# A graph network on one core: a group's layer-norm statistics made one turn later, six pair places, and the span word loaded inside the pair loop

## The chip, the core and the metric

The kernel runs on one core of a Trainium2 chip. The metric is the device time of one execution in microseconds (us), the median of three runs. The engines are TensorE (PE; its weight loads are listed as PEld), VectorE (DVE), ScalarE (ACT), GpSimd (POOL) and SyncE (SP). A letter q behind an engine (DVEq, PEldq) marks what its sequencer does: register arithmetic, branches, register loads, issuing of transfers.

## What is computed

```python
agg = jax.ops.segment_sum(x[src], dst, num_segments=N)      # 6250 nodes, 200000 edges, sorted by dst
h = jax.nn.relu(agg @ W_rel + b_rel + x @ W_root)           # 256 -> 512
gates = h @ W_ih.T + b_ih + b_hh                            # 512 -> 4 * 512
i, f, g, o = jnp.split(gates, 4, axis=-1)
c = jax.nn.sigmoid(i) * jnp.tanh(g)
h_lstm = jax.nn.sigmoid(o) * jnp.tanh(c)
y = h_lstm @ W_fc + b_fc                                    # 512 -> 256
x = _layernorm(x + y, axis=-1)
```

The destinations are drawn as 6250 times a uniform number squared, so low nodes have many edges and high nodes few.

## The kernel before

**Groups and turns.** The 6250 nodes form 25 groups of 250. The program is one sequence of turns, one for each group, written once for each engine; most turns stand in a loop `period` that runs three times over six turns (turns 5 to 10, 11 to 16, 17 to 22). In turn `n` TensorE sums the neighbours of a new group, multiplies the gates of the group of turn `n-1`, and ends with `last_layer(n-1)` and the hidden layer of the new group. Each turn has four slots `j = 0..3`: `part_sum`, then `gates(n-1, j)` (24 matmuls), then the windows of the slot, or one batch of a dense product.

**Two ways of summing.** The 21 sparse groups (nodes 1000 and up) are summed from gathered rows: POOL gathers 128 rows a time (L400, four to a step, an index copied for each at L370) into a ring of `RING = 7` steps, and TensorE multiplies them by one-hots that DVE makes (`visit`, L906 and L476). A step may be overwritten only when TensorE has summed it (`steps_summed`), and summed only when it has landed (`gathered`, which SP raises at L339). The four dense groups (nodes 0 to 999) are summed from counts: their nodes form 100 windows of 10 nodes, each of two spans of 5 nodes. For each span a loop runs over the edges, 512 in an iteration. An iteration is a *pair*: DVE makes two one-hot tiles for it (`rel` L892, `hot_lo` L894, `hot_key` L897, in `span`) and TensorE multiplies the one by the other in four matmuls (L451, in `windows`). There are `PAIRS = 4` places for pairs; DVE waits for a place (`pairs_summed`), TensorE for a pair (`pairs_ready`). Spans of low nodes have several pairs, those of turns 5 and later just one.

**The span's bounds.** At each span's start both engines load one packed word of `table` into a register and split it into the loop's bounds:

```python
        def unpack(engine, regs, at):
            packed, first, past = regs
            engine.reg_load(packed, table[0:1, at:at + 1] if isinstance(at, int) else table[0:1, ds(at, 1)])
            engine.reg_alu(first, packed, PACK, ALU.python_divide)
```

The load is L299 in the profile, the arithmetic L300.

**The layer norm.** `norm_stats(n)` on DVE waits for `last_layer(n)` (`y_ready`), adds it to `x_n`, and takes mean and variance; `deviation(n)` on ACT takes the square root, for which ACT loads another table and then its old one again; `normalise(n)` on DVE scales; `store(n)` on ACT sends the rows out. `norm_stats(n - 1)` stands at the end of DVE's turn `n`, `deviation(n - 2)` at the start of ACT's turn, `normalise(n - 2)` in slot 0, `store(n - 2)` in slot 1. `load_xn` may refill `x_n` when `norm_stats` of the group before has read it (`y_sum`), which `last_layer` waits for too.

**The start.** `srcT` and `dstT` land in SBUF as int32. DVE counts edges into the table, then splits pieces of `x` into high and low parts; POOL waits for the table's head (`table_ready`), copies indices and gathers the first seven steps raw from `x` (L385), and DVE splits these too (`split_gathered`) before turn 0. No order is planned at run time: each engine does what its program lists, and waits.

## Time and profile before

| | before |
|---|---|
| median of 3 runs (lowest, highest) | 1830.2 us (1822.73, 1832.34) |
| profiled execution, its own time | 1824.41 us |
| its span | 1822.5 us |
| busy PE, POOL, DVE, ACT | 1513.5, 1281.0, 815.9, 418.5 us |
| mean granted TensorE clock | 0.91 |
| DMA | 319.14 MB, 175 GB/s on average |

The span lies 1.9 us below the execution's own time. A busy time is a sum over the whole span, and stretches with different limits stand in it side by side, so the rows below are taken by stretch.

### The profile page before, as it was taken

Reading aid. Unit: us, or ns where it says so; the run is one execution under the profiler, and the core shown is the slowest. Engines: PE = TensorE matmul, PEld = TensorE weight load, DVE = VectorE, ACT = ScalarE, POOL = GpSimd, SP = SyncE. Lnnn points to the kernel's source line nnn. Section 1 sums busy time; section 2 is a strip of 40 time slices with the busy share of each in tenths; the row PEclk is TensorE's granted clock in tenths of the full one; section 3 lists DMA queues with packets and bytes.
Section 4 is the critical chain, followed back from the end, with each engine's and each line's share of the span. In section 5 each row is a group of like instructions: output and inputs, shape, how many; then the busy total and the mean of one; then the engine's idle time right before and its main releaser. Section 6 shows DMA issues by size and latency. Waiting matters only on the chain.

```text
span 1822.5 us, 31499 instructions
## 1 busy us (share of the span) xinstructions
PE 1513.5 (83%) x6882; PEld 1213.0 (67%) x6883; DVE 815.9 (45%) x1763; ACT 418.5 (23%) x743; POOL 1281.0 (70%) x1926
## 2 busy tenths in 40 slices
PE   0157688697988898788998889899988888999997
PEld 0023355486767676667887667688876676888886
DVE  8877666431322654531324565422244654222332
ACT  0001021110112332220222333212223332222333
POOL 5875877777777877877777668776763668656640
PEclk9976677698988998889999999999998998999999
DMA  9563555576766555567766445576652455766540
GB/s 342 209 233 87 150 161 145 157 225 207 215 195 180 162 162 165 161 198 223 223 206 180 138 133 166 160 246 217 203 155 77 133 146 161 225 189 177 150 122 18
DMA packets 131966, 319.14 MB, mean 175 GB/s; under 512 B 17295, under 2 KB 68268, under 8 KB 130198
## 3 DMA queue, kind: packets, MB, share of 16 engines
q0 software_dynamic: 75264, 245.95, 46.4%
q10 hardware_dynamic: 52632, 54.80, 9.5%
q1 hardware_dynamic: 3936, 16.62, 2.4%
q8 instruction: 82, 1.34, 0.3%
q14 instruction: 52, 0.43, 0.1%
HBM read 298.10 MB, written 19.20 MB: 174 GB/s over the span
## 4 chain that ended last, share of the span: by engine, by line
PE 48%; POOL 21%; issue 19%; DVE 4%; DMA 3%; DVEq 3%; POOLq 1%; ACT 0%; ACTq 0%; SPq 0%
PE ps_blk L537 20%; POOL rows L400 14%; PE ps_agg L476 9%; PE ps_win L464 6%; POOL idx L370 6%; PE ps_y L545 4%; PE ps_blk L519 3%; PE ps_blk L524 3%; PE ps_tr L451 1%; DMA hot_key<-in_xb 1%; POOL rows L385 1%; PE ps_win L451 1%; DMA rows<-x_parts,idx 1%; POOLq L370 1%; DMA wih_sb<-in_x 1%
## 5 line engine op out<-in xcount | busy, mean ns | idle before, releaser
L400 POOL DMA_INDIRECT rows<-x_parts,idx x924 | 963.5, 1043 | 453.5 <-PE ps_agg L476 157.6
L537 PE MATMUL ps_blk<-cell,wih_sb 128*128 128x250 f32 x2400 | 545.5, 385 | 2.9 <-issue 2.2
L537 PEld LDWEIGHTS ps_blk<-cell,wih_sb 128*128 128x128 f32 x2400 | 464.1, 196 | 69.5 <-issue 8.8
L476 PE MATMUL ps_agg<-rows,onehot 128*125 x1112 | 341.8, 462 | 153.2 <-SPq L339 70.8
L476 PEld LDWEIGHTS ps_agg<-rows,onehot 128*125 128x125 f32 x1112 | 234.1, 216 | 227.5 <-issue 175.9
L906 DVE SCALAR_TENSOR_TENSOR onehot<-iota_f,tile_first,dst_u 128x500 f32 (+1 forms) x278 | 207.0, 746 | 291.7 <-PE ps_agg L476 171.6
L370 POOL COPY idx<-src_sb 128x1 int32 x956 | 264.4, 277 | 16.7 <-issue 9.7
L664 ACT ACTIVATE cell<-ps_blk,bg_sb 128x250 f32<-128x250 f32 x300 | 140.8, 470 | 544.0 <-PE ps_blk L537 470.2
L897 DVE TENSOR_TENSOR hot_key<-iota_h,rel 128x980 f16 x263 | 174.4, 663 | 0.4 <-issue 0.4
L464 PE MATMUL ps_win<-adj,hot_key 128*128 128x250 f32 x784 | 170.7, 375 | 2.4 <-DMA hot_key<-in_xb 1.5
L464 PEld LDWEIGHTS ps_win<-adj,hot_key 128*128 128x128 f32 x784 | 148.0, 190 | 21.6 <-DMA hot_key<-in_xb 4.0
L892 DVE TENSOR_SCALAR rel<-key,span_key x263 | 66.7, 254 | 186.0 <-issue 116.8
L451 PE MATMUL ps_win<-hot_key,hot_lo 128*128 x640 | 113.1, 315 | 34.4 <-issue 20.2
L894 DVE TENSOR_TENSOR hot_lo<-iota_h,src_lo 128x512 f16 x263 | 141.5, 538 | 0.3 <-issue 0.3
L451 PE MATMUL ps_tr<-hot_key,hot_lo 128*128 x412 | 83.2, 312 | 51.3 <-issue 36.3
L451 PEld LDWEIGHTS ps_win<-hot_key,hot_lo 128*128 x640 | 63.7, 100 | 78.2 <-issue 57.5
L519 PE MATMUL ps_blk<-x_t,w_sb 128*128 128x250 f32 x400 | 105.0, 398 | 0.6
L932 DVE TENSOR_TENSOR cell<-cell 128x250 f32<-128x250 f32 x100 | 42.1, 421 | 129.1 <-ACT cell L664 98.1
L451 PEld LDWEIGHTS ps_tr<-hot_key,hot_lo 128*128 x412 | 40.7, 99 | 89.0 <-issue 70.6
L937 DVE TENSOR_TENSOR cell<-cell 128x250 f32<-128x250 f32 x100 | 40.0, 420 | 124.5 <-ACT cell L657 102.8
L524 PE MATMUL ps_blk<-cell,w_sb 128*128 128x250 f32 x400 | 94.6, 378 | 0.0
L639 ACT ACTIVATE adj<-ps_win 128x490 f32<-128x490 f32 x58 | 59.7, 1029 | 146.8 <-PE ps_win L434 90.5
(125 smaller groups left out, 914.2 us busy)
## 6 DMA issues: line engine op xcount, KB each, us to landing
hot_key<-in_xb ACTq DMA_DIRECT2D x28, 896.0 KB
rows<-x_parts,idx POOLq DMA_INDIRECT x924
x_t<-in_xT ACTq DMA_DIRECT2D x25, 250.0 KB
x_n<-in_x ACTq DMA_DIRECT2D x25, 250.0 KB
out<-y ACTq DMA_DIRECT2D x25, 250.0 KB
x_parts<-wih_sb SPq DMA_DIRECT2D x4, 1024.0 KB, 6.8
wih_sb<-in_x ACTq DMA_DIRECT2D x6, 512.0 KB, 9.7
x_parts<-cell SPq DMA_DIRECT2D x2, 1024.0 KB, 7.6
```

The costliest lines, as they stand in the source:

```text
L370: g.tensor_copy(idx[:, k % RING, j:j + 1], src_sb[:, ds(chunk + j, 1)]).then_inc(idx_copied, 1)
L400: g.indirect_dma_start(rows_f[:, k * QC + j, :], None, x_parts, bass.IndirectOffsetOnAxis(ap=idx[:, k, j:j + 1], axis=0)).then_inc(landed[ ...
L451: last = mm(o, hot_lo[:, ds(half, 1), j // 2, :, j % 2].squeeze(1), hot_key[:, ds(half, 1), j // 2, :, j % 2].squeeze(1), start=False, sto ...
L464: last = mm(ps_win[:, c * GN:(c + 1) * GN], xs[:, b, c * P:(c + 1) * P], adj[:, i * X_BATCH + b, :], start=(i == 0 and b == 0 and c == 0), ...
L476: ins = mm(o, onehot[:, hot * QC + j, 0:TN], rows[:, ds(slot + j, 1), :].squeeze(1), start=(first and j == 0), stop=False)
L519: mm(ps_blk[m % BANKS][:, 0:GN], wroot_sb[:, k, m * P:(m + 1) * P], x_t[:, k, :], start=(k == 0), stop=False)
L524: last = mm(ps_blk[m % BANKS][:, 0:GN], wrel_sb[:, k, m * P:(m + 1) * P], agg_t[:, k, :], start=False, stop=(k == KI - 1))
L537: last = mm(o, wih_sb[:, k, col:col + P], h_t[:, k, :], start=(k == 0), stop=(k == KH - 1))
L664: nc.scalar.activation(dst[:, j, :], ps_blk[b % BANKS][:, 0:GN], fn, bias=bg_sb[:, bias + j:bias + j + 1]).then_inc(gate_done, 1)
L894: v.tensor_tensor(hot_lo[:, ds(half, 1), :, :, :].squeeze(1), iota_h[:, 0:P, :].unsqueeze(1).to_broadcast([P, PQ, P, 2]), src_lo[:, ds(c, ...
L897: v.tensor_tensor(hot_key[:, ds(half, 1), :, :, :].squeeze(1), iota_h[:, :, :].unsqueeze(1).to_broadcast([P, PQ, SCOLS, 2]), rel[:, ds(hal ...
L906: v.scalar_tensor_tensor(onehot[:, ds(hot, QC), 0:TN], iota_f[:, 0:TN].unsqueeze(1).to_broadcast([P, QC, TN]), nodes, dst_u[:, ds(c, QC)]. ...
```

## The change

Three edits and what they bring with them.

1. **Statistics a turn later.** On DVE `norm_stats(n - 2)` now stands in slot 0 of turn `n`, behind that slot's one-hots and windows, and `normalise(n - 2)` in slot 1. On ACT `deviation(n - 2)` and `load_xn(n - 1)` move behind slot 0, `store(n - 2)` to slot 2.
2. **Six pair places** instead of four. The room comes from the sources: `src_sb` (int32) becomes `src_u` (uint16), made by one DVE copy from a landing place in the last slot of the ring `rows`. POOL waits for that copy (`src_short`) before its first index, and in the start's seventh step for DVE's two other reads of the landing place (`src_read`).
3. **The word loaded inside the loop.** `unpack` no longer loads. Each iteration of the pair loop loads the word of the *next* span (`load_span`), on TensorE behind the fourth matmul, on DVE between `hot_lo` and the wait for `rel`; the first word is loaded before turn 0. A span with several pairs loads the same word several times.

```diff
-PAIRS = 4
+PAIRS = 6
...
-T_COLS = T_SPAN + SPANS
+T_COLS = T_SPAN + SPANS + 1
...
-        src_sb = sb("src_sb", [P, CHUNK_COLS], i32)
+        src_u = sb("src_u", [P, CHUNK_COLS], u16)
...
+        src_i = flat[:, (RING - 1) * QC * D_ROW:(RING - 1) * QC * D_ROW + CHUNK_COLS].bitcast(i32)
...
-        def unpack(engine, regs, at):
+        def load_span(engine, regs, at):
+            engine.reg_load(regs[0], table[0:1, at:at + 1] if isinstance(at, int) else table[0:1, ds(at, 1)])
+
+        def unpack(engine, regs):
             packed, first, past = regs
-            engine.reg_load(packed, table[0:1, at:at + 1] if isinstance(at, int) else table[0:1, ds(at, 1)])
             engine.reg_alu(first, packed, PACK, ALU.python_divide)
...
-            pool.wait_ge(edges_in, 32)
+            pool.wait_ge(src_short, 1)
...
             def copy_index(chunk, k, j):
-                g.tensor_copy(idx[:, k % RING, j:j + 1], src_sb[:, ds(chunk + j, 1)]).then_inc(idx_copied, 1)
+                g.tensor_copy(idx[:, k % RING, j:j + 1], src_u[:, ds(chunk + j, 1)]).then_inc(idx_copied, 1)
...
+                if k == RING - 1:
+                    pool.wait_ge(src_read, 2)
...
+            load_span(pe, pe_regs, T_SPAN)
...
-                        first, past = unpack(pe, pe_regs, at)
+                        first, past = unpack(pe, pe_regs)
                         with pe.Fori(first, past, QC):
...
                             last.then_inc(pairs_summed, 1)
+                            load_span(pe, pe_regs, at + 1)
                             next_pair(pe, pair_0, place, more_places)
...
             def turn(n, g, g1=None, g2=None, t=None, parts=ALL_PARTS, dense=False, w=None, wins=(0, 0, 0, 0), node=0, k=None, batches=()):
-                if g2 is not None:
-                    deviation(n - 2)
                 load_xt(n, g)
                 if batches:
                     load_batch(k, batches[0])
-                if g1 is not None:
-                    load_xn(n - 1, g1)
                 for j in range(KH):
...
-                    if j == 1 and g2 is not None:
+                    if j == 0 and g2 is not None:
+                        deviation(n - 2)
+                    if j == 0 and g1 is not None:
+                        load_xn(n - 1, g1)
+                    if j == 2 and g2 is not None:
                         store(n - 2, g2)
...
             dve.sem_inc(table_ready, 1)
+            dve.wait_ge(edges_in, 32)
+            v.tensor_copy(src_u[:, :], src_i).then_inc(src_short, 1)
             split_pieces(POOL_PIECES, PARTS)
...
+            load_span(dve, dve_regs, T_SPAN)
...
-                first, past = unpack(dve, dve_regs, at + T_SPAN)
+                first, past = unpack(dve, dve_regs)
...
+                    load_span(dve, dve_regs, at + (T_SPAN + 1))
                     dve.wait_ge(rel_made, s + 1)
...
                     windows_at(w, wins, j)
                     if j == 0 and back >= 2:
+                        norm_stats(n - 2)
+                    if j == 1 and back >= 2:
                         normalise(n - 2)
...
                     out_gate(n - 1, 3)
-                    norm_stats(n - 1)
...
             n = GROUPS - 1
+            norm_stats(n - 1)
             normalise(n - 1)
```

**The pair loop on TensorE**, at the step from the first span of a window to its second. MATMUL is the last or first of a pair, ISA a fused piece of register arithmetic, L306 (L311 after) advances the place. Before:

```order
L451 MATMUL ps_win<-hot_key,hot_lo 128x245
L306 ISA
L446 COMPARE_AND_BRANCH
L299 TENSOR_LOAD table
L300 ISA
L446 UNCONDITIONAL_BRANCH
L447 ISA
L451 ISA [waits pairs_ready]
```

Now:

```order
L459 MATMUL ps_win<-hot_key,hot_lo 128x245
L301 TENSOR_LOAD table
L311 ISA
L454 COMPARE_AND_BRANCH
L305 ISA
L454 UNCONDITIONAL_BRANCH
L455 ISA
L459 ISA [waits pairs_ready]
```

The load moved from behind the loop's closing branch to ahead of it, so that it runs in every iteration and not in every span.

**The pair loop on DVE**, from the second tile of a pair to the next span. Before:

```order
L894 ISA
L894 TENSOR_TENSOR hot_lo<-iota_h,src_lo 128x512
L897 ISA [waits rel_made]
L897 TENSOR_TENSOR hot_key<-iota_h,rel 128x980
L306 ISA
L888 COMPARE_AND_BRANCH
L299 TENSOR_LOAD table
L300 ISA
L888 UNCONDITIONAL_BRANCH
```

Now:

```order
L906 ISA
L906 TENSOR_TENSOR hot_lo<-iota_h,src_lo 128x512
L301 TENSOR_LOAD table
L910 ISA [waits rel_made]
L910 TENSOR_TENSOR hot_key<-iota_h,rel 128x980
L311 ISA
L900 COMPARE_AND_BRANCH
L305 ISA
L900 UNCONDITIONAL_BRANCH
```

Here the load now stands ahead of the issue of `hot_key`.

**DVE from one turn to the next**, where the turn begins with a tile's one-hots. Before, the statistics lay between the last product of a turn and the next turn:

```order
L937 TENSOR_TENSOR cell<-cell 128x250 [waits tanh_c_done]
L940 ISA
L941 TENSOR_TENSOR x_n<-x_n,bfc_sb 125x512 [waits xn_in]
L942 REGISTER_ALU
L945 ISA [waits y_free,y_ready]
L946 TENSOR_TENSOR y<-ps_y,x_n 125x512 [waits ln]
L947 REGISTER_ALU
L949 BN_STATS stats<-y 125x6 [waits y_sum]
```

Now the next turn's one-hots follow the last product at once:

```order
L950 TENSOR_TENSOR cell<-cell 128x250 [waits tanh_c_done]
L925 ISA
L925 TENSOR_LOAD table
L925 ISA x2
L927 ISA
L933 UNCONDITIONAL_BRANCH [waits hot_used]
L933 ISA
L919 ISA [waits hot_used]
L919 ISA
L919 SCALAR_TENSOR_TENSOR onehot<-iota_f,tile_first,dst_u 128x4x125
```

and the statistics stand behind the loops of the slot's spans:

```order
L900 COMPARE_AND_BRANCH
L953 ISA
L954 TENSOR_TENSOR x_n<-x_n,bfc_sb 125x512 [waits xn_in]
L958 ISA [waits y_free,y_ready]
L959 TENSOR_TENSOR y<-ps_y,x_n 125x512 [waits ln]
L960 REGISTER_ALU
L962 BN_STATS stats<-y 125x6 [waits y_sum]
```

The wait for `y_ready` has thus gone from ahead of a turn's first one-hots to behind them and the pairs.

## Rows read from the trace of the kernel before

**Rows 1.** Busy time by stretch: us, then PE, PEld, DVE, ACT, POOL, PEclk, DMA.

```profile
152.00:862.00 710.00, 582.11 (x2556) 448.58 (x2555) 317.99 (x692) 145.95 (x247) 559.29 (x845) 0.85 0.61 177
862.00:1822.00 960.00, 886.67 (x4166) 742.75 (x4166) 375.18 (x864) 268.23 (x492) 624.12 (x964) 0.96 0.56 164
```

**Rows 2.** TensorE's waits in 153 to 857 us: total, times, longest.

```profile
PE ps_agg L476 <- SPq L339: 68.1, 17, 6.0
```

**Rows 3.** POOL's waits in 862 to 1822 us.

```profile
POOL rows L400 <- PE ps_agg L476: 132.2, 18, 24.9
```

**Rows 4.** The chain that ended last, at 857 us: start, us, what.

```profile
857.29 5.11 DMA rows<-x_parts,idx
```

**Rows 5.** POOL's timeline, turn 0: start, us, instruction, idle before it.

```profile
152.43 0.97 POOL L400 DMA_INDIRECT rows<-x_parts,idx  x1 [19.43 <-PE ps_agg L476]
```

**Rows 6.** TensorE's timeline, turn 0, slot 0, and its first visit behind.

```profile
121.56 1.00 PE L451 MATMUL ps_win<-hot_key,hot_lo 128*128 x4 [0.20 <-issue]
122.74 1.00 PE L451 MATMUL ps_win<-hot_key,hot_lo 128*128 x4 [0.18 <-issue]
124.45 1.00 PE L451 MATMUL ps_win<-hot_key,hot_lo 128*128 x4 [0.71 <-DVE hot_key L897]
...
150.71 7.40 PE L476 MATMUL ps_agg<-rows,onehot 128*125 x24 [1.19 <-DVE onehot L906]
```

**Rows 7.** The pair matmuls of 110 to 150 us: count, duration min/median/max.

```profile
L451 PE MATMUL ps_win<-hot_key,hot_lo x92: 269/397/411, 109.9 to 149.1; 128*128 x92
...
L451 PE MATMUL ps_tr<-hot_key,hot_lo x32: 384/407/411, 131.0 to 140.5; 128*128 x32
```

**Rows 8.** The register loads of L299, whole span: duration ns min/median/max.

```profile
L299 DVEq TENSOR_LOAD <-table x200: 306/311/1847, 105.3 to 1526.2; - x100
L299 PEldq TENSOR_LOAD <-table x200: 296/302/323, 108.6 to 1537.9; - x100
```

**Rows 9.** The chain in 107 to 160 us, at a span's start on DVE.

```profile
119.86 0.32 DVEq L299
120.21 0.22 DVEq L300
```

**Rows 10.** DVE's timeline: first tiles of two following pairs of one span.

```profile
109.82 0.23 DVE L892 TENSOR_SCALAR rel<-key,span_key  x1
...
110.99 0.23 DVE L892 TENSOR_SCALAR rel<-key,span_key  x1
```

**Rows 11.** Costliest groups: index copies, pairs on DVE, the cast of `dstT`.

```profile
L370 POOL COPY idx<-src_sb 128x1 int32 x956 | 264.4, 277 | 16.7 <-issue 9.7
...
L897 DVE TENSOR_TENSOR hot_key<-iota_h,rel 128x980 f16 x263 | 174.4, 663 | 0.4 <-issue 0.4
...
L859 DVE CAST dst_u<-hot_key 128x1568 uint16<-128x1568 int32 x1 | 1.0, 976 | 0.2 <-DVE table L856 0.2
```

**Rows 12.** DVE's timeline, the last raw step.

```profile
101.06 0.69 DVE L772 TENSOR_SCALAR adj<-rows 128x1024 int32<-128x1024 int32 x1 [8.10 <-DMA rows<-in_x,idx]
```

**Rows 13.** TensorE's groups in 862 to 1822 us: busy, mean ns, idle before.

```profile
L451 PE MATMUL ps_tr<-hot_key,hot_lo 128*128 x176 | 32.3, 280 | 23.4 <-issue 16.0 <-DVE hot_key L897 7.4
L451 PE MATMUL ps_win<-hot_key,hot_lo 128*128 x224 | 32.1, 280 | 6.9 <-issue 4.3 <-DVE hot_key L897 2.6
```

**Rows 14.** TensorE's timeline in turns 11 and 12.

```profile
990.05 5.67 PE L476 MATMUL ps_agg<-rows,onehot 128*125 x16 [5.58 <-DVE onehot L906]
...
1031.00 0.89 PE L451 MATMUL ps_win<-hot_key,hot_lo 128*128 x4 [1.03 <-DVE hot_key L897]
...
1053.07 3.12 PE L476 MATMUL ps_agg<-rows,onehot 128*125 x12
```

**Rows 15.** DVE's timeline in the same turns.

```profile
1027.47 0.66 DVE L897 TENSOR_TENSOR hot_key<-iota_h,rel 128x980 f16 x1
...
1051.79 2.30 DVE L906 SCALAR_TENSOR_TENSOR onehot<-iota_f,tile_first,dst_u 128x500 f32 x3 [1.36 <-issue]
```

**Rows 16.** ACT's timeline in turn 10: the first of two table loads.

```profile
948.70 1.28 ACT L675 ACT_TABLE_LOAD   x1
```

More of the change, by code:

```diff
@@ L242, in gnn_kernel @@
         edges_in = sem("edges_in")
+        src_short = sem("src_short")
+        src_read = sem("src_read")
         bias_in = sem("bias_in")
@@ L316, in _ @@
             sp.dma_start(dst_next, dstq[QPC * CHUNK:(QP + 1) * QPC * CHUNK].rearrange("(p e) -> p e", p=QP)[:, 0:CHUNK]).then_inc(dstq_in, 16)
-            sp.dma_start(src_sb[:, :], srcT).then_inc(edges_in, 16)
+            sp.dma_start(src_i, srcT).then_inc(edges_in, 16)
             sp.dma_start(dst_i, dstT).then_inc(edges_in, 16)
@@ L857, in _ @@
             dve.sem_inc(spans_ready, 1)
-            dve.wait_ge(edges_in, 32)
             v.tensor_copy(dst_u[:, :], dst_i).then_inc(setup, 1)
-            v.tensor_scalar(src_part, src_sb[:, :], P - 1, None, ALU.bitwise_and).then_inc(setup, 1)
-            v.tensor_scalar(src_high, src_sb[:, :], P.bit_length() - 1, None, ALU.logical_shift_right).then_inc(setup, 1)
-            n_setup[0] += 3
+            v.tensor_scalar(src_part, src_i, P - 1, None, ALU.bitwise_and).then_inc(src_read, 1)
+            v.tensor_scalar(src_high, src_i, P.bit_length() - 1, None, ALU.logical_shift_right).then_inc(src_read, 1)
+            n_setup[0] += 1
             dve.wait_ge(setup, n_setup[0])
+            dve.wait_ge(src_read, 2)
             link(v.tensor_copy(src_lo[:, :], src_part))
```

## The prediction

> **What bounds the kernel now.** I read the busy times by stretch first, then the waits of the two engines that pass rows to each other, then the chain, and last the timelines around the edits. The reader is to see a kernel with three limits in a row.
>
> From 152 to 862 us POOL's gathering sets the pace: TensorE waits 68.1 us in 17 places for gathered steps [rows 2], and its busy time is 582.11 of 710 us [rows 1]. From 862 us on TensorE is the limit: busy 886.67 of 960 us [rows 1], while POOL waits 132.2 us for it to release the ring [rows 3]. The chain changes over at the landing of 857.29 us, which is the last gather that TensorE had to wait for [rows 4]. What a faster or slower TensorE is worth must therefore be asked twice. Before 152 us it is a third thing. POOL stands still for 19.43 us until 152.43 [rows 5], because the ring is full and TensorE is in the windows of slot 0; its next visit starts at 150.71 [rows 6]. Everything up to 862 us follows from that release, at POOL's pace. So a delay in slot 0 of turn 0 goes into the end whole; a delay in the windows of turns 1 to 8 is taken up by the waits of [rows 2]; one after 862 us counts again.
>
> What sets TensorE's pace in the windows? Within a span pairs follow at 122.74 - 121.56 = 1.18 us, and across a span's start at 124.45 - 122.74 = 1.71 us [rows 6]. The four matmuls do not explain it: they keep the array busy for 1.00 us of it, and they take 0.40 us each only because the clock is down (269 ns at best, [rows 7]). DVE does not either: the profile names `hot_key` as releaser at places, but the pair summed at 1031.00 us was made by 1027.47 + 0.66 = 1028.13 [rows 14, 15]. That leaves TensorE's own sequencer, with register arithmetic for each matmul, a branch, and at a span's start the load and the split of a word.
>
> **The load inside the loop.** The load takes 302 ns on TensorE and 311 ns on DVE, 200 times each [rows 8]. After it the next piece of arithmetic starts at 120.21, when the load of 119.86 had ended at 120.18 [rows 9]. Every load here is followed by an instruction that needs its value, so the trace cannot say whether an independent one would have passed it. I bound it: nothing at all if the sequencer goes on at once; 0.30 + 0.05 = 0.35 us each if it stands. I take the upper end, because the record of the load is a closed 0.3 us with the next record right behind it, as with any arithmetic. (Estimate: the 0.05 is the gap of 0.03 of [rows 9], rounded up for TensorE.)
>
> Loads in the loop are as many as pairs, 263 [rows 11], instead of 200. A span with one pair keeps its one load, only at the other end of the pair: no change of the sequencer's sum. A span with more pays for each further pair. In slot 0 of turn 0 there are 92 + 32 = 124 matmuls [rows 7], so 31 pairs, in 3 windows = 6 spans: 25 more loads, 25 x 0.35 = **+8.8 us**, all ahead of the release at 152.43. DVE has the same load, but its pairs follow at 110.99 - 109.82 = 1.17 us [rows 10], and part of the load falls into its wait for `rel`; at worst 1.52 against TensorE's 1.53, so it doesn't bind first. Taking the whole difference of a span's start (0.53) for a load would give 13 us, none if loads overlap 0: the ends of this term are 0 and +13.
>
> The other 63 - 25 = 38 further loads lie in the rest of turns 0 and 1, where POOL sets the pace: 38 x 0.35 = 13 us hidden by [rows 2]'s 68.1. If that cover were gone they would cost those 13.
>
> After 862 us there are 176 + 224 = 400 pair matmuls, 100 pairs, all of one-pair spans [rows 13]: 0 if the sequencer stands at a load.
>
> The Trainium skill has two sentences on such loads. "Runtime: NRT & Kernel Launch", section "Instruction fetch mechanics", gives about 200 ns for each register even in bulk, a round trip, where stores are sent off without waiting; by 200 ns the 25 loads would cost 5 us and the sum would be 6 instead of 10. No run here shows a bulk load; the single ones are at 302 ns.
>
> **The start.** DVE's copy to uint16 is put ahead of its piece work and POOL's first index waits for it. The nearest row is the cast of `dstT`, as wide: 0.98 us [rows 11]. POOL has nothing to do before its first index (9.7 us idle there, [rows 11]), and DVE stands for the raw gathers' last landing at 101.06 after 8.10 us [rows 12], so POOL's delay is the chain's: **+1.1 us** with the semaphore. Ends: 0 and +3. The index copies then read uint16 instead of int32. No row has a conversion on POOL; a copy of one column takes 277 ns [rows 11], 845/2 = 422 of them stand in the stretch where POOL is the limit [rows 1]. I take 0, since for one element a partition the data can hardly matter; a fifth more each would be 0.055 x 422 = 23 us, a doubling five times that. The wait for `src_read` comes in the seventh raw step, long after DVE's reads: 0.
>
> **Statistics a turn later.** This takes a wait and some 3 us of work on DVE from ahead of a turn's first one-hots. But TensorE doesn't stand there: it begins turn 12 at 1053.07 without idle time [rows 14], with the one-hot begun at 1051.79 and 2.30/3 = 0.77 us long [rows 15]. Its cover was thin, 0.5 us, and gets thick; worth 0 on the path. Behind the statistics in slot 0 now queue the one-hots and pairs of slot 1, but they start from a lead of six pairs, and TensorE has 24 gate matmuls ahead of it. ACT's square root brings its two table loads, 1.28 us each [rows 16], between the gates of slots 0 and 1. TensorE needs the banks of slot 1's first gate back three blocks of eight matmuls later, about 5 us, longer than 2.8: 0. `x_n` and `y` move with their readers by the same slot: 0.
>
> **Six places.** They let DVE run further ahead of a TensorE that doesn't wait for it: 0, and they are what hides the statistics.
>
> **Sum:** 8.8 + 1.1 = +9.9 us. On the profiled execution 1824.4 + 9.9 = 1834.3 us; on the median of the runs shown, 5.8 us above it, 1830.2 + 9.9 = **1840 us**. Half a per cent (9 us) is about what a measurement of this kernel tells from no change, so the forecast is a hair beyond it.
>
> **Rivals.**
> *A, loads overlap (other side).* If the sequencer issues the load and goes on, slot 0 costs nothing, and after 862 us each of the 100 pairs gets up to 0.3 us back where the sequencer is the limit. Idle before pair matmuls there is 23.4 + 6.9 = 30.3 us [rows 13]. It decides as soon as more than a third of a load is hidden there, for 100 x 0.3 = 30 outweighs 25 x 0.35. Less what the gates' queue hid already, -26: 1830 - 26 + 1 = **1805 us**. For it: the word isn't needed for a whole branch. Against it: the closed record of [rows 8, 9]. The Trainium skill's "DMA: Bandwidth & Descriptors", section "Latency and other measured facts", says that the compiler unrolls `tensor_load` fourfold to spread a floor of about 600 ns, which speaks for overlap; the trace's 302 ns is half that floor, and no run here shows two in a row.
> *B, the moved statistics do pay.* At two period starts in TensorE's stretch, such as 990.05, it stood 5.58 us with a one-hot named as releaser [rows 14]. Such a start costs 1.19 us elsewhere [rows 6]. If DVE was the reason, 2 x 4.4 = 9 us come back and nothing is left: **1831 us**, "same". Against it: it happens only where the loop `period` jumps back, and TensorE jumps there too, whatever DVE does.
> *C, the index copy is slower.* +10 and +23: **1863 us**.
> *D, statistics or square root come late*, so that `normalise` holds `cell_product` and with it ACT and the last layer: a table load of 1.28 in each of some 8 turns, **1850 us**. Against: the lead of six pairs.
>
> **How the numbers follow.** The forecast 0.45 (its own range 1833 to 1849: ends 0 and +13 with the start's 0 to 3, and 3 us of scatter); A 0.20; B, or other small gains against the loads, 0.22; C 0.06; D 0.07. Slower by over 0.5%: three quarters of the forecast's 0.45, and C and D: 0.46, which I cut to 0.44 as A's and D's effects can meet. Same: the rest of the forecast and most of B: 0.31. Faster: A and some of B: 0.25. The range goes from A's 1803 to a little above D, 1853; below lies about 0.06, above 0.08.
>
> **What would show it.** The step is right if the loads' count is 263 (and one) on each engine at some 0.30 us, if pairs within a span in turn 0 follow at 1.53 instead of 1.18 us, those across a start still at 1.7, POOL's wait before its thirteenth step grows from 19.4 to about 28, and all later landmarks (the changeover near 857) come 10 us later. Rival A shows as 1.2 us within spans and under 1.5 across. The statistics are right if TensorE starts its turns without idle time as before. Wrong would make me, first, a load that costs TensorE nothing; second, a limit in slot 0 other than its sequencer.

## The result and the profile after

| | before | changed |
|---|---|---|
| median (lowest to highest), 4 runs each, same chip | 1828.11 us (1822.73 to 1832.34) | 1847.72 us (1845.93 to 1851.52) |
| profiled execution, its span | 1824.41, 1822.5 us | 1848.81, 1847.0 us |
| mean granted TensorE clock | 0.91 | 0.902 |

The ratio is 1.0105, 95% interval [1.008, 1.013]: the change costs 19.6 us. I had forecast a loss of 9.9. The direction and the first mechanism hold, the size is half of what came. I read the profile after in the order of the forecast: first the loads, then slot 0 of turn 0, then where the rest came in.

Register loads of the changed kernel (count, ns min/median/max):

```profile
L301 PEldq TENSOR_LOAD <-table x264: 296/302/487, 57.4 to 1561.9; - x132
L301 DVEq TENSOR_LOAD <-table x264: 300/305/940, 73.9 to 1546.9; - x132
```

TensorE's timeline in slot 0 of turn 0, against [rows 6]:

```profile
121.57 1.00 PE L459 MATMUL ps_win<-hot_key,hot_lo 128*128 x4 [0.58 <-DVE hot_key L910]
123.15 1.00 PE L459 MATMUL ps_win<-hot_key,hot_lo 128*128 x4 [0.58 <-DVE hot_key L910]
...
126.27 1.00 PE L459 MATMUL ps_win<-hot_key,hot_lo 128*128 x4 [0.54 <-issue]
127.96 1.00 PE L459 MATMUL ps_win<-hot_key,hot_lo 128*128 x4 [0.69 <-issue]
...
159.77 1.64 PE L485 MATMUL ps_agg<-rows,onehot 128*125 x3 [1.12 <-issue]
```

POOL, as it goes on after that slot, against [rows 5]:

```profile
161.49 0.96 POOL L407 DMA_INDIRECT rows<-x_parts,idx  x1 [30.12 <-PE ps_agg L485]
```

The loads are 263 and one more at 0.30 us. Within a span pairs follow at 123.15 - 121.57 = 1.58 us, where it was 1.18; across a span's start still at 1.69. The first visit behind the slot starts at 159.77 instead of 150.71, and POOL at 161.49 instead of 152.43: **+9.06 us at both**. From the first pair matmul of slot 0 to the last it is 48.5 us where it was 39.6: 8.9 us for 25 more loads, 0.36 us each.

Waits of the changed kernel, TensorE's in 153 to 862 us (against [rows 2]):

```profile
PE ps_agg L485 <- SPq L344: 50.3, 13, 6.5
```

and POOL's in 862 to 1845 us (against [rows 3]):

```profile
POOL rows L407 <- PE ps_agg L485: 158.8, 22, 26.8
```

Busy time by stretch (against [rows 1]; us, PE, PEld, DVE, ACT, POOL, clock, DMA):

```profile
153.00:862.00 709.00, 580.19 (x2558) 444.62 (x2558) 328.21 (x695) 146.53 (x248) 553.53 (x836) 0.85 0.61 176
862.00:1845.00 983.00, 901.62 (x4182) 756.14 (x4181) 379.88 (x864) 267.10 (x492) 623.40 (x973) 0.94 0.55 161
```

In the second stretch TensorE is busy for 15 us more with nearly the same matmuls (4182 against 4166), and its granted clock is 0.94 instead of 0.96. The end of turn 8 comes 9.3 us later than before (895.4 and 886.1 us), the end of the last turn 24.3 us later. So the forecast fits up to turn 8 and misses some 15 us behind it. Profiles scatter by a few us like all runs: the two profiled executions lie 24.4 us apart, the medians 19.6. A second execution of the same program, the profile of e4 below, ends its last turn 20.6 us later than before, and I give its lengths beside those of the first.

**Where the 15 us are.** A turn's end is taken from the trace as the end of its hidden layer's matmuls. The three dense turns in the loop (10, 16, 22) grow from 36.3, 36.3, 35.3 to 37.9, 37.9, 37.2 us: +5.1. The six turns with windows (11, 12, 13, 17, 18, 19) grow from 404.6 to 417.4 us in sum: +12.8. All others together are -2.8 from turn 9 on. In e4 the dense turns grow by the same 5.1, but the six turns with windows only by 5.4 (to 410.0), and all others are at +0.2. So the 12.8 are not a property of the kernel; about half of them belong to the one execution.

For the dense turns, ACT in turn 10 of the changed kernel:

```profile
964.89 1.28 ACT L684 ACT_TABLE_LOAD   x1
966.18 0.20 ACT L684 ACTIVATE std<-ve 125x2 f32<-125x2 f32 x1
966.40 1.28 ACT L673 ACT_TABLE_LOAD   x1
```

DVE there:

```profile
966.42 0.17 DVE L972 RECIPROCAL r<-std 125x2 f32<-125x2 f32 x1 [13.16 <-ACT std L684]
...
967.41 0.77 DVE L983 TENSOR_SCALAR y<-y,mv,rstd 125x256 f32<-125x256 f32 x2
...
969.19 2.47 DVE L919 SCALAR_TENSOR_TENSOR onehot<-iota_f,tile_first,dst_u 128x500 f32 x3 [0.67 <-issue]
```

and TensorE:

```profile
963.77 5.66 PE L546 MATMUL ps_blk<-cell,wih_sb 128*128 128x250 f32 x26
970.14 3.39 PE L485 MATMUL ps_agg<-rows,onehot 128*125 x12 [0.71 <-DVE onehot L919]
```

`normalise(n - 2)` now stands in slot 1, and the next one-hots of a dense turn are those of slot 2 (its slot 1 has none), so they queue behind it. It waits for a square root that ACT reaches only behind slot 0's gates. DVE had nothing to do for 13.16 us, then it did the normalising just before TensorE wanted the one-hots: they begin at 969.19, and TensorE stands from 969.43 to 970.14 for the first of them. This is my rival D, small, and by way of the one-hots, not of `cell_product`. (The Trainium skill, "ScalarE: Activation LUTs", section "What ACT_TABLE_LOAD costs", gives 2.66 us for each switch of tables, of which 1.38 a drain. The loads agree with its 1283 ns; but both switches and the root took 967.68 - 964.89 = 2.79 us here, so no such drain stood behind either.)

For the turns with windows, TensorE in turn 12 shows one of 24 such slots (each `...` leaves out rows without idle time), before:

```profile
1061.51 1.05 PE L451 MATMUL ps_win<-hot_key,hot_lo 128*128 x8
...
1064.25 0.89 PE L451 MATMUL ps_tr<-hot_key,hot_lo 128*128 x4 [1.04 <-issue]
1065.22 0.17 PE L434 MATMUL ps_tr<-zero_bf 128*128 128x1 bf16 x1
1066.67 3.31 PE L476 MATMUL ps_agg<-rows,onehot 128*125 x12 [1.27 <-DVE onehot L906]
```

and changed:

```profile
1074.18 1.05 PE L459 MATMUL ps_win<-hot_key,hot_lo 128*128 x8
...
1076.47 0.90 PE L459 MATMUL ps_tr<-hot_key,hot_lo 128*128 x4 [0.66 <-issue]
1077.95 0.17 PE L442 MATMUL ps_tr<-zero_bf 128*128 128x1 bf16 x1 [0.57 <-issue]
1079.39 4.52 PE L485 MATMUL ps_agg<-rows,onehot 128*125 x12 [1.27 <-issue]
```

The load has left the gap ahead of the fourth pair (1.04 to 0.66) and stands behind it (0 to 0.57): 0.19 us more idle time, where I had said "no change of the sequencer's sum". The sum is the same, but the first load of a slot used to be issued while the gates' matmuls were still queued, and the last one of a slot now stands where nothing is queued. The same shows in the sums behind 862 us, for the matmul that closes a window in the bank `ps_tr`: 2.0 us of idle time ahead of it in all before,

```profile
L434 PE MATMUL ps_tr<-zero_bf 128*128 128x1 bf16 x22 | 3.8, 171 | 2.0
```

and 13.5 us in the changed kernel,

```profile
L442 PE MATMUL ps_tr<-zero_bf 128*128 128x1 bf16 x22 | 3.8, 172 | 13.5 <-issue 13.5
```

while the idle time ahead of the pairs' matmuls falls from 30.3 [rows 13] to 22.4 us. In sum TensorE is idle in the six turns for 60.6 us before and 65.1 changed. This part repeats: four kernels without the load in TensorE's loop (before, e1, e9, e10) have 60.1 to 60.6 us, the five with it (changed, e2, e3, e4, e6) and e7, which has the load behind the loop, have 63.2 to 66.9.

And the visit behind it, the same twelve matmuls, takes 4.52 instead of 3.31 us. The granted clock of TensorE over that visit (us, busy, clock, DMA) was full before:

```profile
1066.60:1069.90 3.30, 3.23 (x12) 1.00 0.58 164
```

and changed for most of it at the lower of the two levels, 1.2 instead of 2.4 GHz:

```profile
1079.40:1083.70 4.30, 4.30 (x12) 0.63 0.65 186
```

The windows of turns 11, 12 and 13 show both parts; before (us, PE, PEld, DVE, ACT, POOL, clock, DMA):

```profile
984.50:1053.40 68.90, 55.83 (x268) 44.62 (x269) 37.11 (x87) 21.37 (x34) 44.90 (x64) 0.90 0.49 138
1053.40:1123.30 69.90, 59.51 (x290) 46.31 (x289) 39.71 (x91) 21.79 (x35) 55.04 (x78) 0.95 0.54 155
1123.30:1186.70 63.40, 56.66 (x270) 45.08 (x269) 33.31 (x78) 19.80 (x33) 49.49 (x75) 0.95 0.58 166
```

and changed:

```profile
994.30:1066.40 72.10, 57.18 (x268) 45.81 (x269) 40.06 (x92) 21.27 (x35) 41.33 (x60) 0.86 0.43 124
1066.40:1138.90 72.50, 61.24 (x289) 48.45 (x288) 42.25 (x95) 21.75 (x35) 55.62 (x80) 0.91 0.55 157
1138.90:1204.50 65.60, 58.42 (x270) 47.23 (x269) 32.05 (x72) 19.74 (x33) 49.80 (x75) 0.90 0.57 158
```

Of the 8.0 us that these three turns grow (202.2 to 210.2), 4.8 are busy time of the same matmuls at a lower granted clock (0.90, 0.95, 0.95 to 0.86, 0.91, 0.90), and 3.2 are idle.

The busy part does not repeat as the idle part does. Over all six turns TensorE is busy for 342.1 to 348.6 us in the profiles of the four kernels without the load in the loop, and for 343.3 to 352.2 in those of the six with it (343.9 before, 352.2 changed, 346.6 in e4, 343.3 in e2). Where the clock falls for some us differs from one execution to the next. Over whole executions the clock does go with the load: its mean over a kernel's runs is 0.907 to 0.911 for the four and 0.902 to 0.906 for the six. Slot 0 of turn 0, where the clock is low in all of them, is itself longer in the six, so the means do not say how much of it lies behind 862 us.

### The profile page after: what moved, and what is told of

It reads as the page before. It is cut to its first block, busy times and chain, and to the rows that moved or that the text cites. A ratio compares the mean times of both kernels' runs of the same rounds, so it can differ in the third digit from the quotient of the medians.

```text
span 1847.0 us, 31619 instructions
## 1 busy us (share of the span) xinstructions
PE 1523.2 (82%) x6882; PEld 1220.2 (66%) x6883; DVE 833.1 (45%) x1764; ACT 417.0 (23%) x743; POOL 1272.5 (69%) x1926
## 4 chain that ended last, share of the span: by engine, by line
PE 44%; POOL 25%; issue 21%; DVE 3%; DMA 3%; DVEq 2%; POOLq 2%; ACT 0%; ACTq 0%; SPq 0%
POOL rows L407 17%; PE ps_blk L546 16%; PE ps_agg L485 9%; POOL idx L375 7%; PE ps_win L473 5%; PE ps_blk L528 4%; PE ps_y L554 3%; PE ps_blk L533 3%; PE ps_win L459 2%; DMA rows<-x_parts,idx 2%; PE ps_tr L459 1%; POOL rows L392 1%; DVE hot_key L910 1%; POOLq L375 1%; DMA wih_sb<-in_x 1%
## 5 line engine op out<-in xcount | busy, mean ns | idle before, releaser
L407 POOL DMA_INDIRECT rows<-x_parts,idx x924 | 943.7, 1021 | 489.6 <-PE ps_agg L485 196.2
L485 PE MATMUL ps_agg<-rows,onehot 128*125 x1112 | 346.1, 466 | 143.2 <-SPq L344 63.1
L375 POOL CAST idx<-src_u 128x1 int32 x956 | 284.7, 298 | 13.2 <-issue 10.8
L473 PEld LDWEIGHTS ps_win<-adj,hot_key 128*128 128x128 f32 x784 | 148.1, 190 | 19.6 <-DMA hot_key<-in_xb 3.0
L459 PE MATMUL ps_tr<-hot_key,hot_lo 128*128 x412 | 79.4, 310 | 46.6 <-issue 26.3
```

What stands on the lines that cost most here:

```text
L375: g.tensor_copy(idx[:, k % RING, j:j + 1], src_u[:, ds(chunk + j, 1)]).then_inc(idx_copied, 1)
L407: g.indirect_dma_start(rows_f[:, k * QC + j, :], None, x_parts, bass.IndirectOffsetOnAxis(ap=idx[:, k, j:j + 1], axis=0)).then_inc(landed[ ...
L459: last = mm(o, hot_lo[:, ds(half, 1), j // 2, :, j % 2].squeeze(1), hot_key[:, ds(half, 1), j // 2, :, j % 2].squeeze(1), start=False, sto ...
L473: last = mm(ps_win[:, c * GN:(c + 1) * GN], xs[:, b, c * P:(c + 1) * P], adj[:, i * X_BATCH + b, :], start=(i == 0 and b == 0 and c == 0), ...
L485: ins = mm(o, onehot[:, hot * QC + j, 0:TN], rows[:, ds(slot + j, 1), :].squeeze(1), start=(first and j == 0), stop=False)
```

## The experiments

"POOL on" is the time at which POOL goes on after turn 0's slot 0; "dense" the lengths of turns 10, 16 and 22; "clock" the granted one from 862 us to the end. Each ratio is to the kernel before on the same chip.

| run | ratio [95%] | POOL on | dense | clock |
|---|---|---|---|---|
| before | | 152.43 | 36.3, 36.3, 35.3 | 0.96 |
| changed | 1.0105 [1.008, 1.013] | 161.49 | 37.9, 37.9, 37.2 | 0.94 |
| e1 load at the span's start | 1.0004 [0.9986, 1.0022] | 152.40 | as changed | 0.96 |
| e2 load alone | 1.0081 [1.0051, 1.0111] | 161.90 | as before | 0.95 |
| e3 statistics back | 1.0069 [1.0049, 1.0089] | 161.76 | as before | 0.96 |
| e4 (repeats the changed kernel) | 1.0124 [1.0099, 1.0149] | 161.71 | as changed | 0.95 |
| e5 two loads | 1.0564 [1.0523, 1.0605] | 173.70 | as changed | 0.92 |
| e6 in the loop on TensorE alone | 1.0093 [1.0061, 1.0126] | 160.15 | as changed | 0.95 |
| e7 behind the loop on TensorE | 1.006 [1.0034, 1.0086] | 155.50 | as changed | 0.95 |
| e8 words in the gates | 0.9747 [0.9716, 0.9778] | 149.80 | as before | 0.97 |
| e9 normalise behind | 1.0013 [0.9996, 1.003] | 153.11 | as before | 0.96 |
| e10 six places alone | 0.9987 [0.9966, 1.0009] | 153.50 | as before | 0.96 |
| e11 splits in the gates too | 0.9726 [0.9707, 0.9746] | 149.53 | as before | 0.98 |
| e12 e11 with late statistics | 0.9763 [0.9738, 0.9788] | 151.06 | 36.3, 36.3, 35.3 | 0.99 |

**e1: the changed kernel with the load at the span's start again.** The edit on TensorE; DVE's is the same:

```diff
+                        load_span(pe, pe_regs, at)
                         first, past = unpack(pe, pe_regs)
...
-                            load_span(pe, pe_regs, at + 1)
```

> The changed kernel with the word loaded at each span's start again (200 loads instead of 264); statistics a turn later and six places stay. Theory L (the load in the loop costs it all, 9 us in slot 0 of turn 0 and the rest in the window turns after 862 us, where it moves idle time behind a slot's last pair and keeps the clock low): within 5 us of the kernel before, first slot over by about 151 us. Theory S (the moved statistics cost the part after 862 us, through the square root that now holds the one-hots of dense turns, and through a changed rhythm): 9 to 10 us under the changed kernel, so 8 to 12 us over the kernel before, with turns 11, 12, 17, 18 still 2 to 3 us longer. Under both the dense turns 10, 16 and 22 stay 1.5 us longer each.

1829.83 us against 1829.13. Pairs within a span are back at 1.18 us, here TensorE in turn 0, and POOL goes on at 152.40:

```profile
121.53 1.00 PE L459 MATMUL ps_win<-hot_key,hot_lo 128*128 x4 [0.20 <-issue]
122.71 1.00 PE L459 MATMUL ps_win<-hot_key,hot_lo 128*128 x4 [0.18 <-issue]
124.41 1.00 PE L459 MATMUL ps_win<-hot_key,hot_lo 128*128 x4 [0.70 <-DVE hot_key L908]
```

The load in the loop carries nearly all of the loss. The dense turns stay long, so their 5 us are the statistics' part and are not the load's.

**e2: the kernel before with the load in the loop alone** (the diff's `load_span` lines and nothing else).

> The kernel before with nothing but the word loaded inside the loop. Theory L: 14 to 20 us over the kernel before, pairs 1.58 us apart within a span, turns 11, 12, 17, 18 longer by 2 to 3 us, dense turns as before. Theory S: 9 us over, all of it by 160 us, turns from 10 on as long as before.

1845.8 us against 1829.13 (the ratio says 15 us, the medians 17), without the statistics or the six places. POOL on at 161.90, dense turns at 36.3.

**e3: the changed kernel with the statistics back where they were.** Edit, on DVE, with ACT's calls moved back to match:

```diff
                     if j == 0 and back >= 2:
-                        norm_stats(n - 2)
-                    if j == 1 and back >= 2:
                         normalise(n - 2)
...
+                    norm_stats(n - 1)
```

> The changed kernel with the statistics, the square root and the store where they were; load in the loop and six places stay. Theory L: as the changed kernel less the dense turns' 3 x 1.6 us, so 13 to 16 us over the kernel before. Theory S: 9 to 10 us over the kernel before.

1840.98 us. Between e3 (1.0069) and the changed kernel (1.0105 and, as e4, 1.0124) the statistics cost 0.36 to 0.55% with the load in the loop, 7 to 10 us; e3's interval stays clear of e4's and just overlaps that of the changed kernel. With the load at the span's start they cost 1.0004 - 0.9987 = 0.17%, 3 us, which the intervals of e1 and e10 cannot tell from nothing.

**e4 and e5: a second load in each iteration on TensorE.**

> The changed kernel with the same load issued twice in TensorE's loop (DVE's loop unchanged). If the sequencer stands for each load: pairs 1.93 us apart within a span in turn 0, 31 x 0.36 = 11 us later release, and 100 x 0.36 = 36 us more after 862 us, some 45 us over the changed kernel in all. If an independent load is passed, the second costs under 0.1 us: less than 10 us over it.

In e4 nothing read the second load's register, and no instruction was left of it: the run has 264 loads on TensorE. It says nothing on the load's price and is a repeat of the changed kernel. e5 makes the span's split use it:

```diff
-            engine.reg_add(past, past, packed)
+            engine.reg_add(past, past, packed if again is None else again)
...
                             load_span(pe, pe_regs, at + 1)
+                            load_span(pe, [spare], at + 1)
```

> The changed kernel with a second load of the same word in TensorE's loop, into a register of its own that the split uses, so that both stay (528 loads on TensorE, 264 on DVE). If the sequencer stands for each: pairs 1.58 + 0.36 = 1.94 us apart within a span of turn 0, the release of POOL some 11 us after the changed kernel's 161.5, and 100 x 0.36 = 36 us more after the changeover: about 45 us over the changed kernel, 1890 to 1900 us. If the second is passed while the first is under way: pairs less than 0.1 us further apart, under 10 us over the changed kernel.

It has 528 loads. TensorE in turn 0:

```profile
121.77 1.00 PE L461 MATMUL ps_win<-hot_key,hot_lo 128*128 x4 [0.92 <-DVE hot_key L913]
123.71 1.00 PE L461 MATMUL ps_win<-hot_key,hot_lo 128*128 x4 [0.94 <-issue]
125.65 1.00 PE L461 MATMUL ps_win<-hot_key,hot_lo 128*128 x4 [0.94 <-DVE hot_key L913]
```

1.18, 1.58, 1.94 us with none, one and two loads: a load in the loop costs 0.36 to 0.40 us, and a second one directly behind the first is no cheaper. POOL goes on at 173.70, 12.2 us after the changed kernel. Of these, 11.0 lie between the first and the last pair matmul of slot 0 (59.5 against 48.5 us), for 31 more loads: 0.36 us each again. The whole, 1935.18 us, misses my expectation by some 40 us. It is 87 us above the changed kernel, close to 263 x 0.36 = 95, but not for that reason. In the profiles turn 8 ends 44.9 us later than in the changed kernel, 33 of them behind slot 0, where I had expected all to be hidden: turns 1, 5 and 6, which hold most of the pairs there, are 31 us longer, and TensorE's waits for gathered steps fell only from 50.3 to 36.1 us. The six turns with windows take 40.4 us more, 20.0 of them idle, so that of 100 x 0.36 = 36 a part was hidden there, and 20.5 in longer matmuls; the clock behind 862 us fell to 0.92. Their 372.7 us of busy time lie well outside the 342 to 352 of all kernels with one load or none in the loop.

**e6: the load in the loop on TensorE, at the span's start on DVE.**

> The changed kernel with the load in the loop on TensorE alone; DVE loads at each span's start as before. If TensorE's sequencer is what the load costs: as the changed kernel within 4 us (15 to 20 us over the kernel before), release of POOL at 161.5 us. If DVE's load mattered: near the kernel before, within 6 us of it.

1844.93 us; POOL on at 160.15. The loss is TensorE's. The 1.3 us by which POOL goes on earlier are not DVE's loads: slot 0 takes the same 48.7 us from its first pair matmul to its last and only begins earlier, at 108.24 instead of 109.80. Where TensorE has its own load in the loop, DVE's are hidden behind it.

**e7: TensorE's load once for each span, behind the loop.**

```diff
-                            load_span(pe, pe_regs, at + 1)
                             next_pair(pe, pair_0, place, more_places)
+                        load_span(pe, pe_regs, at + 1)
```

> The changed kernel with TensorE's load once behind each span's loop instead of in every iteration: 200 loads, but still between a span's last pair and what follows, so that a window's closing matmul waits for it. It parts the number of loads from their place. If only the number counts: release of POOL back at 152.5 us and the kernel before's time within 4 us. If the place counts too (idle time gathered behind a slot's last pair, clock low for longer): release at 152.5 us, but turns 11, 12, 17, 18 still 2 to 3 us longer, 7 to 10 us over the kernel before.

1838.32 us: POOL goes on at 155.50, 6 us earlier than in the changed kernel but 3 us later than I expected if the number of TensorE's loads were all. These 3 us are DVE's: its load is still in its loop, and with TensorE's out of the way its pairs set the pace, at 1.41 us instead of 1.20:

```profile
127.69 1.00 PE L459 MATMUL ps_win<-hot_key,hot_lo 128*128 x4 [0.41 <-DVE hot_key L910]
129.10 1.00 PE L459 MATMUL ps_win<-hot_key,hot_lo 128*128 x4 [0.41 <-issue]
```

This kernel, with no more loads on TensorE than before, is still 0.56% (10 us) over e1. It differs from e1 in the place of TensorE's load by one branch (for a slot, in whether its first load is issued under the gates' queue or its last one stands at the open end) and in DVE's loads. The idle time of the six turns is 63.7 us, against 60.2 in e1 and 65.1 changed, so the load's place costs some us there without any further load. How the rest of the 10 divides, no run shows: e6 bounds DVE's loads only where TensorE's load is in the loop too.

**e8: no load in the windows.** The kernel before with six places, and the words of a slot loaded into eight registers between the matmuls of `gates` ahead of it:

```diff
-            def gates(n, j):
+            def gates(n, j, w=None, n_windows=0):
...
+                        if which * KH + k < 2 * n_windows:
+                            load_word(w, which * KH + k)
...
-                        windows(w, wins[j])
+                        windows(w, wins[j], ahead=not first or j == 0)
```

> The kernel before with six places (statistics where they were), and on TensorE the words of a slot's spans loaded into registers of their own between the gate matmuls ahead of the slot, where some 3 us of queued matmuls cover the sequencer; turn 0 loads its first slot's words before its first tile. If the load is a standing wait of the sequencer that only the place can hide: 100 x 0.3 to 0.4 us back after the changeover, 20 to 30 us under the kernel before, and the gap before a slot's fourth pair down from 1.03 to about 0.6 us. If DVE's pairs (1.83 us each) bind once TensorE is faster: under 10 us back, with waits for hot_key in place of issue.

1783.85 us, 45 us less than before and more than the 20 to 30 that I expected; my count had left out the loads before 862 us, and in the profile turn 8 ends 11.8 us earlier. TensorE in slot 0 of turn 11 and at the gates of slot 1:

```profile
994.35 1.05 PE L467 MATMUL ps_win<-hot_key,hot_lo 128*128 x8
...
995.37 1.04 PE L467 MATMUL ps_tr<-hot_key,hot_lo 128*128 x8
...
996.27 5.65 PE L553 MATMUL ps_blk<-cell,wih_sb 128*128 128x250 f32 x24
```

The gap of 1.04 us is gone; the 24 gate matmuls of slot 1, at full clock in both, take 5.65 instead of 5.33 us with four loads among them, so 1.2 us of loads cost 0.3 there. The gates of slot 0, which follow a visit, hold four loads too and take 5.23 us as before. Turns 11, 12, 17 and 18 go from 68.9, 69.9, 68.0, 69.7 to 64.0, 63.2, 63.8, 64.2 us.

**e9: e1 with the normalise behind slot 1's one-hots** in turns without a tile in that slot:

```diff
-                    if j == 1 and back >= 2:
+                    if j == (1 if parts[1] is not None or parts[2] is None else 2) and back >= 2:
```

> The changed kernel with the load at the span's start again (as in e1, 1.0004), and one order more: in the turns that multiply counts (dense turns, no tile in slot 1) the normalise stands behind slot 1's one-hots, and the store a slot later. Theory: in turns 10, 16 and 22 the one-hots waited behind a normalise that waited for ACT's square root; those turns fall back from 37.9, 37.9, 37.2 to about 36.3 us, and the kernel is 4 to 5 us faster than e1: ratio about 0.998. Rival: the dense turns are longer because ACT's table loads stand between the gates; then they stay at 37.9 and the time stays at 1.000.

DVE now makes the one-hots first:

```profile
957.62 2.46 DVE L917 SCALAR_TENSOR_TENSOR onehot<-iota_f,tile_first,dst_u 128x500 f32 x3 [1.27 <-issue]
959.99 0.16 DVE L970 RECIPROCAL r<-std 125x2 f32<-125x2 f32 x1
```

The dense turns fall to 36.3, 36.3 and 35.3 us, as the theory had it. The time does not follow: 1.0013 against e1's 1.0004, where about 0.998 was expected; the two intervals leave room for some 3 us of gain. The mechanism of the dense turns is shown, its 5 us are not in the medians.

**e10: six places and short sources alone.**

> The kernel before with six pair places and the sources as uint16, nothing else. My forecast's terms: places 0, start +1.1 us measured as 0. Theory: 1.000 (within 0.3 per cent), all landmarks within 1 us. Rival: DVE's lead of six pairs already gives something back in the slots after 862 us, where TensorE's hot_key waits are 10 us in all: up to 5 us faster, 0.997; this would also take 5 us of what e8 gained.

1822.27 against 1826.08 us, 0.9987 [0.9966, 1.0009]: nothing, or up to 6 us of gain; a loss from the start or from the index copies could be 2 us at most.

**e11: e8 with the splits in the gates too.**

```diff
                 load_span(pe, pe_regs, w0 * 2 + (T_SPAN + i))
+                packed, first, past = bounds[i]
+                pe.reg_alu(first, packed, PACK, ALU.python_divide)
+                pe.reg_alu(past, first, -PACK, ALU.mult)
+                pe.reg_add(past, past, packed)
```

> e8 (words loaded between the gates' matmuls, 0.975) with the split of each word (three pieces of register arithmetic) in the gates as well, so that a span starts with nothing but its loop's branch. Theory: TensorE's sequencer sets the pace between spans and has slack in the gates, where 8 matmuls take 1.8 us and their issue less: 200 splits of 0.2 us, half of them behind 862 us: 15 to 25 us faster than e8, ratio about 0.964. Rival 1: the gates' own issue is used up by the loads (they grew from 5.33 to 5.7 us), so each split only moves: within 5 us of e8. Rival 2: DVE's pairs, at about 1.2 us each, become the limit: TensorE waits for hot_key, and the time stays as well.

1774.82 us, the fastest of all: 51 us under before (1826.08). Against e8 it is 9 us by the medians and 4 by the ratios, whose intervals overlap; the expected 15 to 25 did not come. TensorE in the same place of turn 11:

```profile
988.29 1.05 PE L472 MATMUL ps_win<-hot_key,hot_lo 128*128 x8
...
989.31 1.05 PE L472 MATMUL ps_tr<-hot_key,hot_lo 128*128 x8
...
990.22 6.29 PE L558 MATMUL ps_blk<-cell,wih_sb 128*128 128x250 f32 x24
```

The windows of this slot hold no gap, as in e8, but the gates of slot 1 go from 5.65 to 6.29 us, at full clock: four loads cost 0.3 us there, four splits on top of them 0.64. This is rival 1 in part: the sequencer's slack under the gates is used up by the loads, and a split there is mostly moved, not hidden.

**e12: e11 with the change's statistics, in e9's order.**

> e11 with the change's statistics a turn later, in e9's order. Theory: with the sequencer's load gone from the windows the cover of DVE's work at a turn's first one-hots gets thinner, so that moving the statistics is worth something here where it was worth nothing before: 2 to 6 us faster than e11. Rival: DVE has over 40 per cent of idle time in every turn and the one-hots keep their lead: no difference within 2 us, or 3 us slower by the dense turns if e9 shows that its order does not help.

1778.25 us, 0.9763 against 0.9726: not faster, as the rival said. Its profiled span (1773.7 us) equals e11's (1773.1): turn 8 ends 5.1 us later and what follows is 4.5 us shorter, each in one execution. The 3 us between the medians have no place in the trace that I could name.

## Why the prediction was right, and by how much it was off

**What bounds the kernel, and the load that stands in the sequencer's way: right.** The pairs' pace is TensorE's sequencer's; 1.58 us within a span against my 1.53, release +9.06 against +8.8 us, and no overlap of loads (e5). POOL's wait became 30.1 us where I had said about 28, because it began earlier. Rival A (1805 us) had been that they overlap; it falls with e1 and e5. The price of one load, 0.36 us on average over slot 0 (8.9 us for 25, and 11.0 for 31 in e5), is what I had put at 0.35. The Trainium skill's "Runtime: NRT & Kernel Launch", section "Instruction fetch mechanics", gives about 200 ns for a register; the measured 302 decides, and by 200 ns the sum would have been further off.

**The other 38 extra loads hidden before 862 us: right.** TensorE's waits for gathered steps fell from 68.1 [rows 2] to 50.3 us, and turn 8 ends 9.3 us late, as much as the release. In e3, e4 and e6 it ends 9.6 to 9.9 us late; only in e2 is it 15.9, with POOL going on 9.5 us late.

**The start, +1.1 us: open, and 0 in the changed kernel's profile.** There POOL's first index comes at 32.75 instead of 31.98 us and its first gather at 36.74 instead of 36.23, but the first pair matmul at 109.80 instead of 109.87. In the other kernels with the copy that matmul comes between 108.24 (e6) and 110.57 us (e10), which is more scatter than the term is large. Rival C falls: the index cast takes 298 ns where the copy took 277 [rows 11], while the gather's mean was 1021 ns against 1043, and e10 shows no loss.

**"After 862 us ... 0 if the sequencer stands at a load": this is the step that failed.** I counted loads, and their number there is indeed the same, but I gave each load one price wherever it stands. The old place hid the first load of each slot under the queue of gate matmuls; the new place has the last one of each slot stand in the open instead. That is 24 loads in six turns; by [rows 8] they could cost 24 x 0.3 = 7.2 us, and the idle time of the six turns grew by 4.5 (3 to 6 in the other kernels with the load in the loop). I also took TensorE's busy time as fixed: it grew by 8.2 us in those turns in the profile of the changed kernel, but by 2.7 in the repeat e4, by nothing in e2, and by 4.7 in e1, which has the load where it was. So what the clock's share of the loss is stays open. e2 prices the load without the statistics: 15 to 17 us, of which 9 are slot 0 and 6 to 8 everything behind it. That the idle time brings the lower clock is argued from their going together (0.98 in e11, with 28 us of idle time in the six turns, 0.92 in e5, with 85, against 0.96 and 61 before); no run changed one without the other.

**"Longer than 2.8: 0" for the square root: wrong.** I checked ACT against TensorE's banks and not DVE against ACT. `normalise` made slot 2's one-hots of the dense turns queue behind it, +5.1 us in the profile; removing that alone (e9) gave nothing measurable. What is shown of the statistics is 3 us that can't be told from nothing without the load in the loop, and 7 to 10 with it. Rival D (1850 us, 0.07) was thus nearer than its chance said. Rival B is not seen: the stop at the loop's jump back stays, turns 11 and 17 have the same idle time in e1 (13.6 and 13.3 us) as before (13.1 and 13.2).

**Six places: 0 is right** (e10); what they are worth in e8 and e11 was not tried apart.

In sum, by the profile of e4: 9.9 us up to the end of turn 8, 5.4 in the turns with windows, 5.1 in the dense turns and 0.2 elsewhere are 20.6, against 19.6 between the medians. By the runs: 15 to 17 for the load (e2) and 3 to 10 for the statistics (e1 with e10, e3 with the changed kernel). The forecast had 8.8 of it right, by its mechanism. That the rest came to only some 10 us, so that the time still lies between 1803 and 1853 us, was not foreseen; that part is luck. How the statistics' part divides between the dense turns and the clock stays open.

## What to carry to other kernels

Price a register load, like any instruction of a sequencer that sets the pace, by what is queued ahead of it at its place and not by its count: under 24 gate matmuls four of them cost nothing to 0.3 us (5.23 and 5.23, 5.33 and 5.65 us), at the open end of a slot or in a loop of 1.2 us each costs 0.36 to 0.40. So values that a loop's bounds need belong between the matmuls ahead of the loop; a loss of 1% with the load in the loop stands against a gain of 2.5% (e8) to 2.7% (e11) with the words loaded there. And when a wait is moved later in an in-order queue, list what stands behind it at its new place and who wants that, not only what it frees at the old one. A difference of a few us between two profiles is worth a repeat of the same program before it is explained: here it took 7 of 12.8 us away.

## What the runs showed that I had not expected

- A load of one word from SBUF holds a sequencer's following arithmetic even where that does not need the word: 1.18, 1.58 and 1.94 us for a pair with 0, 1 and 2 loads (e1, changed, e5).
- The same twelve matmuls took 3.31 and 4.52 us in the same slot of turn 12, and the granted clock from 862 us on was 0.98 with 5 us of idle time in each of turns 11 and 12 (e11), 0.96 with 13 and 10 (before), 0.94 with 15 and 11 (changed). Yet two executions of the same program differ by 5.6 us in the busy time of the six turns (352.2 and 346.6).
- 263 loads of 0.30 us, added once more, cost 87 us, of which some 20 are longer matmuls (e5 against the changed kernel).
- DVE's load in its own loop costs 0.2 us a pair once TensorE's is out of the way (1.41 against 1.20 us, e7), and nothing beside it (e6).
